# Graph message passing on one core: a tile of each pair made from columns on chip, joins in batches of twelve

## The reference

```python
msg_in = concatenate([nodes[row], nodes[col], edge_features], axis=-1)
messages = relu(msg_in @ mW1 + mb1) @ mW2 + mb2
aggregated = segment_sum(messages, col, num_segments=12500)
upd_in = concatenate([nodes, aggregated], axis=-1)
out = layernorm(nodes + relu(upd_in @ uW1 + ub1) @ uW2 + ub2)
```

## Time and profile before

| | us |
|---|---|
| median of 3 executions (2004.75 to 2006.22) | 2005.02 |
| the profiled execution | 2009.95 |
| its span, first to last instruction | 2008.1 |

### The profile page before, as it was taken

The page is one execution under the profiler, slowest core; times in us unless marked ns, Lnnn a source line. Parts: engine busy times, 40 slices in busy tenths (PEclk is TensorE's granted clock), DMA queues, the critical chain, the costliest instruction groups (busy, mean ns, idle before and its releaser), DMA issues.

```text
span 2008.1 us, 34318 instructions
## 1 busy us (share of the span) xinstructions
PE 1444.5 (72%) x8744; PEld 1325.3 (66%) x8744; DVE 1113.1 (55%) x4860; ACT 902.5 (45%) x6697; POOL 1479.6 (74%) x1576
## 2 busy tenths in 40 slices
PE   6866586777777666777667677768678767767778
PEld 6865575776667665667667666757667666666666
DVE  5545555555555555555555555555555555555553
ACT  3234453554454453454444444444444444444543
POOL 5677777777777777777777777777777777777773
PEclk9877777777777777877787778677776878787876
DMA  9554444444444444444344444445444444444441
GB/s 246 147 130 103 114 121 110 109 122 116 102 122 119 101 121 115 104 122 120 99 122 121 99 121 120 102 118 121 100 120 120 100 120 121 105 116 120 106 108 32
DMA packets 102730, 232.68 MB, mean 116 GB/s; under 512 B 47018, under 2 KB 63223, under 8 KB 89917
## 3 DMA queue, kind: packets, MB, share of 16 engines
q1 hardware_dynamic: 42532, 124.03, 24.4%
q0 software_dynamic: 49952, 100.83, 20.8%
q10 hardware_dynamic: 10046, 5.59, 1.2%
HBM read 220.66 MB, written 9.60 MB: 115 GB/s over the span
## 4 chain that ended last, share of the span: by engine, by line
POOL 73%; issue 24%; DMA 1%; PE 1%; POOLq 0%; ACT 0%; DVE 0%; DVEq 0%
POOL gath L798 71%; POOL hid L782 1%; DMA hid<-in_x_dram,idx_all 1%; POOL raw_x L782 1%; PE ps_sum L934 0%; DMA gath<-table_src,idx_all 0%; PE ps_pre L981 0%; PE ps_pre L987 0%; PE ps_pre L986 0%; PE ps_pre L997 0%; PE ps_pre L996 0%; POOLq L126 0%; DVE hid L1304 0%; PE ps_node L987 0%; PE ps_node L986 0%
## 5 line engine op out<-in xcount | busy, mean ns | idle before, releaser
L798 POOL DMA_INDIRECT gath<-table_src,idx_all x1513 | 1431.1, 946 | 461.4 <-issue 461.4
L914 PE MATMUL ps_pre<-rhs,lhs 128*128 128x128 f32 x3226 | 605.3, 365 | 531.7 <-DVE lhs L1275 529.0
L914 PEld LDWEIGHTS ps_pre<-rhs,lhs 128*128 128x128 f32 x3226 | 568.4, 273 | 549.3 <-DVE lhs L1275 546.3
L1304 DVE TENSOR_TENSOR hid<-ps_pre,gath 128x1024 f32<-128x1024 f32 x202 | 246.8, 1222 | 719.4 <-DMA gath<-table_src,idx_all 692.5
L520 ACT COPY col_x<-xz 64x1 f32 x5960 | 571.9, 189 | 3.3 <-issue 1.8
L934 PE MATMUL ps_sum<-onehot,hid 128*128 128x96 f32 x3322 | 482.1, 307 | 5.0 <-ACT hid L1105 3.4
L934 PEld LDWEIGHTS ps_sum<-onehot,hid 128*128 128x128 f32 x3322 | 462.5, 222 | 25.3 <-issue 19.5
L1105 ACT ACTIVATE hid<-hid 128x1024 f32<-128x1024 f32 x202 | 212.5, 1052 | 347.4 <-DVE hid L1304 347.2
L543 DVE TENSOR_TENSOR col_x<-xz 64x2 int32 x3366 | 264.2, 148 | 101.2 <-issue 98.5
L1275 DVE TENSOR_SCALAR_CACHE_REDUCE lhs<-lhs,place 96x1024 f32<-96x1024 int32 x208 | 262.5, 1262 | 14.6 <-DMA lhs<-in_dst_dram 14.6
L1067 ACT COPY rhs<-ps_sum 96x128 f32<-96x128 f32 x208 | 53.7, 259 | 354.0 <-DVE xz L1333 353.3
(11 more groups left out here) (136 smaller groups left out, 679.9 us busy)
## 6 DMA issues: line engine op xcount, KB each, us to landing
lhs<-in_dst_dram SPq DMA_DIRECT2D x99, 768.0 KB
lhs<-in_edgeT_dram SPq DMA_DIRECT2D x98, 256.0 KB
gath<-table_src,idx_all POOLq DMA_INDIRECT x1513
table_src<-gath SPq DMA_DIRECT2D x12, 512.0 KB, 8.0
xwin<-in_xT_dram SPq DMA_DIRECT2D x208, 24.0 KB
lhs<-in_dst_dram SPq DMA_DIRECT2D x10, 384.0 KB, 4.6
out_dram<-late_b ACTq DMA_DIRECT2D x48, 64.0 KB, 2.1
xz<-in_xT_dram ACTq DMA_DIRECT2D x4, 512.0 KB, 11.0
```

Source lines behind the costliest of these rows:

```text
L798: pool.indirect_dma_start(gath[0:m, k, j * H:(j + 1) * H], None, table_src, src_by_tile(p, j, m)).then_inc(gathered[k], 16)
L914: mm = nc.tensor.matmul(to[0:m, j * H:(j + 1) * H], lhs[:, k, j * P:j * P + m], rhs[:, k, :], start=True, stop=not by_cols)
L1304: nc.vector.tensor_tensor(hid[:, k, at], ps_pre[k % 2][:, at], gath[:, k, at], ALU.add).then_inc(hsum_made, 1)
```

## The change

Three things change together.

- From pair 11 on every pair has its last tile by columns (`COL_EVERY` 1), and of pairs 16, 20, ..., 204 tile 6 too (`TWO_FROM`, `TWO_EVERY`), in a buffer `col_y` of its own. The columns of tile 6 are put together over the four steps before: in each 8 by ScalarE and 24 by VectorE. Of tile 7 ScalarE now copies 56 and VectorE joins 72.
- VectorE's addition covers only the gathered tiles. ScalarE applies relu to the others straight from PSUM, and TensorE waits for that (`cols_relued`) before it writes that PSUM buffer again. The zeros are no longer needed.
- VectorE's joins come in batches of 12, each with a load of 24 registers: one after the addition, one after onehot, one after the comparison, and the one for tile 6 after the sums.

The column table gets a third plane. POOL's waits between the first six pairs' gathers are left out.

```diff
-COL_EVERY = 2
+COL_EVERY = 1
 COL_TILE = PT - 1
-COL_ACT = 60
-COL_LOADS = (12, 16, 12, 12, 8)
-COL_DVE = 32
+COL_ACT = 56
+COL_LOADS = (12, 16, 12, 8, 8)
+COL_JOINS = (24, 24, 24)
...
+TWO_FROM = 16
+TWO_EVERY = 4
+TWO_TILE = PT - 2
+TWO_STEPS = 4
+TWO_ACT = 8
+TWO_DVE = 24
+TWO_DVE_FROM = TWO_STEPS * TWO_ACT
...
+        col_f = sb("col_f", [P, 3 * TAB])
+        col_tab = sb("col_tab", [P, 3, P], I32)
         col_x = sb("col_x", [D, SLOTS, P])
+        col_y = sb("col_y", [D, 2, P])
...
+        def has_two(p):
+            return TWO_FROM <= p < LAST_PAIR and (p - TWO_FROM) % TWO_EVERY == 0
+        def two_ahead(p):
+            for part in range(TWO_STEPS):
+                if has_two(p + 1 + TWO_STEPS - part):
+                    return p + 1 + TWO_STEPS - part, part
+            return None
...
-            return rows_of(p) if is_last(p) else PT - has_cols(p)
+            return rows_of(p) if is_last(p) else PT - has_cols(p) - has_two(p)
+        def has_psum_rows(p):
+            return has_cols(p) and not is_last(p)
...
+        def load_two_regs(eng, p, start, count):
+            regs = [eng.alloc_register(f"col{next(col_regs)}") for n in range(count)]
+            eng.load(regs, col_tab[p // 2:p // 2 + 1, 2, start:start + count])
+            return regs
...
             pool.wait_ge(idx_first_in, 16)
             for r in range(RAW):
-                if r > 0:
-                    pool.wait_ge(raw_got[r - 1], 16 * PT)
                 for j in range(PT):
                     pool.indirect_dma_start(raw(r, j), None, x, src_by_tile(r, j, P)).then_inc(raw_got[r], 16)
...
                 pe.wait_ge(hsum_made, p - 1)
+                if has_psum_rows(p - 2):
+                    pe.wait_ge(cols_relued, col_batches(p - 2))
                 for j, m in tiles_of(p):
                     by_cols = has_cols(p) and (j == col_tile(p) or j == TILES and is_last(p))
+                    if has_two(p) and j == TWO_TILE:
+                        mm = nc.tensor.matmul(to[0:m, j * H:(j + 1) * H], lhs[:, k, j * P:j * P + m], rhs[:, k, :], start=True, stop=False)
+                        pe.wait_ge(two_act, TWO_STEPS * twos(p))
+                        pe.wait_ge(two_dve, TWO_STEPS * twos(p))
+                        mm = nc.tensor.matmul(to[0:m, j * H:(j + 1) * H], col_y[:, twos(p) % 2, 0:m], w_src[0:D, :], start=False, stop=True)
+                        continue
                     mm = nc.tensor.matmul(to[0:m, j * H:(j + 1) * H], lhs[:, k, j * P:j * P + m], rhs[:, k, :], start=True,
                                           stop=not by_cols)
                     if by_cols:
                         if j == col_tile(p):
                             pe.wait_ge(cols_act, col_batches(p) + is_last(p))
-                            pe.wait_ge(cols_dve, 2 * col_batches(p))
+                            pe.wait_ge(cols_dve, col_batches(p))
...
-                    pe.wait_ge(cols_listed, 2)
-                    for half in range(2):
+                    pe.wait_ge(cols_listed, 4)
+                    for half in range(3):
                         ins = nc.tensor.transpose(ps_node[0:TAB, half * P:(half + 1) * P], col_f[:, half * TAB:(half + 1) * TAB], ident[:, :])
...
             def relu(p, it, k):
                 act.wait_ge(hsum_made, p + 1)
-                h = hid[:, k, 0:rows_of(p) * H]
+                if has_psum_rows(p):
+                    at = slice(gathers_of(p) * H, PW)
+                    nc.scalar.activation(hid[:, k, at], ps_pre[k % 2][:, at], ACT.Relu).then_inc(cols_relued, 1)
+                h = hid[:, k, 0:gathers_of(p) * H]
                 nc.scalar.activation(h, h, ACT.Relu).then_inc(hid_made, 1)
...
                     held = act_regs.pop() + load_regs(act, p + 2, COL_LOADS[0], COL_LOADS[1])
-                    copy_batch(act, nc.scalar.copy, to, 0, held)
+                    copy_batch(act, nc.scalar.copy, col_x[:, to, :], 0, held)
                 window_at(it, k)
                 if has_cols(p + 2):
                     for count in COL_LOADS[2:]:
-                        done = copy_batch(act, nc.scalar.copy, to, start, load_regs(act, p + 2, start, count))
+                        done = copy_batch(act, nc.scalar.copy, col_x[:, to, :], start, load_regs(act, p + 2, start, count))
                         start += count
                     done.then_inc(cols_act, 1)
+                if two_ahead(p):
+                    q, part = two_ahead(p)
+                    held = load_two_regs(act, q, part * TWO_ACT, TWO_ACT)
+                    copy_batch(act, nc.scalar.copy, col_y[:, twos(q) % 2, :], part * TWO_ACT, held).then_inc(two_act, 1)
                 if p + 2 >= COL_FROM and has_cols(p + 3):
                     first_regs(p + 3)
...
                 dve.wait_ge(gathered[k], got(p))
-                if first_cols(p):
-                    dve.wait_ge(gath_zero, zeroed_before(p))
                 if is_last(p):
                     dve.wait_ge(last_made, len(LAST_TILES))
-                at = slice(0, rows_of(p) * H)
+                at = slice(0, gathers_of(p) * H)
                 nc.vector.tensor_tensor(hid[:, k, at], ps_pre[k % 2][:, at], gath[:, k, at], ALU.add).then_inc(hsum_made, 1)
-                if first_cols(p + SLOTS):
-                    dve.wait_ge(hsum_made, p + 1)
-                    nc.vector.memset(gath[:, k, COL_TILE * H:PW], 0.0).then_inc(gath_zero, 1)
...
+            def join_part(p, i):
+                if has_cols(p + 2):
+                    if i == 0:
+                        wait_cols(dve, p + 2)
+                    start = DVE_FROM + sum(COL_JOINS[:i])
+                    done = join_batch(col_x[:, (p + 2) % SLOTS, :], start, load_regs(dve, p + 2, start, COL_JOINS[i]))
+                    if i == len(COL_JOINS) - 1:
+                        done.then_inc(cols_dve, 1)
             def step(it, k):
                 if isinstance(it, int) and (it, k) == (1, 0):
                     relative(1)
+                p = it * SLOTS + k
                 before = pair(it, k, 1)
                 if before and not is_raw(before[0]):
                     add_gathered(*before)
+                join_part(p, 0)
                 if not (isinstance(it, int) and pair(it, k)[0] < 2):
                     onehots(*pair(it, k))
-                p = it * SLOTS + k
                 if p % SLOTS == SLOTS - 1:
                     load_starts(p - SLOTS + 1)
                 at = place_sums(p - 3) if p >= 3 else None
...
-                if has_cols(p + 1):
-                    to, start = (k + 1) % SLOTS, DVE_FROM + COL_DVE
-                    done = join_batch(col_x[:, to, :], start, load_regs(dve, p + 1, start, P - start))
-                    done.then_inc(cols_dve, 1)
-                if has_cols(p + 2):
-                    wait_cols(dve, p + 2)
+                join_part(p, 1)
                 after_this = pair(it, k, -1)
                 if after_this and after_this[0] >= 2:
                     turned(*after_this)
+                join_part(p, 2)
                 if pair(it, k, 3):
                     add_sums(*pair(it, k, 3), at)
-                if has_cols(p + 2):
-                    to = (k + 2) % SLOTS
-                    held = load_regs(dve, p + 2, DVE_FROM, COL_DVE)
-                    join_batch(col_x[:, to, :], DVE_FROM, held).then_inc(cols_dve, 1)
+                if two_ahead(p):
+                    q, part = two_ahead(p)
+                    start = TWO_DVE_FROM + part * TWO_DVE
+                    join_batch(col_y[:, twos(q) % 2, :], start, load_two_regs(dve, q, start, TWO_DVE)).then_inc(two_dve, 1)
```

More of the change, by code:

```diff
@@ L279, in gnn_kernel @@
         rings_made = sem("rings_made")
[L280 removed]
+        cols_relued = sem("cols_relued")
+        two_act = sem("two_act")
+        two_dve = sem("two_dve")
         gathered = [sem(f"gathered{i}") for i in range(SLOTS)]
@@ L457, in col_tile, with twos @@
             return LAST_ROWS if is_last(p) else COL_TILE
+        def has_two(p):
+            return TWO_FROM <= p < LAST_PAIR and (p - TWO_FROM) % TWO_EVERY == 0
+        def twos(p):
+            return sum(has_two(q) for q in range(p + 1))
+        def two_ahead(p):
[3 more added lines that the diff above has]
+            return None
         def gathers_of(p):
-            return rows_of(p) if is_last(p) else PT - has_cols(p)
+            return rows_of(p) if is_last(p) else PT - has_cols(p) - has_two(p)
+        def has_psum_rows(p):
+            return has_cols(p) and not is_last(p)
         def got(p):
@@ L471, in col_batches @@
             return sum(has_cols(q) for q in range(COL_FROM, p + 1))
-        def col_before(p):
-            return next((q for q in range(p - SLOTS, COL_FROM - 1, -SLOTS) if has_cols(q)), None)
-        def first_cols(p):
-            return has_cols(p) and col_before(p) is None
-        def zeroed_before(p):
-            return sum(first_cols(q) for q in range(p + 1))
         def two_of(p):
@@ L511, in column, with copy_batch @@
```

(14 more changed lines are left out.)

16 lines of the change are left out of this document (7 added, 9 removed).

## The result

The changed kernel takes 2027.26 us (median of nine runs, 2015.02 to 2032.15), the kernel before beside it 2006.22: the ratio is 1.0099, with a 95% interval of 1.0077 to 1.0121. It is 1% slower. The forecast was 1987 us and faster; the time lies within its range, on the side of the first rival. The profiled execution took 2026.47 us, its span is 2024.6.

A forecast was written before the change was run, and what follows sets the result against it. GpSimd's gathers were taken to bound the kernel at 9.38 us a pair, then VectorE's queue at 9.37; an earlier start and shorter end gave 18 us off the median of 2005.02, so 1987 us, range 1935 to 2045.

The forecast's parts named there:

- the first rival: VectorE's and ScalarE's register loads collide: one VectorE load of four 0.22 us longer, step 9.59, 2029 us; 22 in 100.
- The bound moves from GpSimd to VectorE's queue: From pair 11 on: the step goes from a POOL of 9.38 us to a VectorE queue of 9.37.
- POOL's floor of 8.44 us a step: GpSimd's gathers after the change: 6.75 a steady pair at 1.2505 us each, 0.94 us below before.
- The datapath at 7.5 us a step: VectorE's joins and other operations sum to 7.5 us a pair, without the queue's loads and issue.
- the shared port's rival: GpSimd shut out during VectorE's joins: 11.9 us a step, over 2470 us; 1 in 100.
- The queue's sum, 9.37: VectorE's queue a pair: loads 6.52, issue 2.24, and smaller terms for arithmetic, holes, window starts and node stage.
- Its note that each load lies behind a large operation: VectorE: each load follows a large operation and 12 joins, about 1.75 us of datapath work, hiding most of it.
- four loads of 24: 4 x 1.63 = 6.52: VectorE's queue: four 24-register loads a pair at 1.63 us each, bounds 1.5 and 1.85.
- The start: Up to pair 11: addition for pair 6 stays at 102.79, then 34.3 us to pair 11's at 137.1, not 151.5.
- The 0.60 for faster: Whole kernel: chance 0.60 that the change measures faster, against 0.10 the same and 0.30 slower.

The follow-up runs named there:

- the runs with 4 and 32 registers: Changed kernel with each VectorE batch load cut from 24 registers to 4, serving all 12 joins: 1802 us; or lengthened to 32, 8 of them unused: 2423 us.
- the layout in one half: Changed kernel with the seventh tile's table rows placed so VectorE and ScalarE nearly always load from the same half of the partitions: 1992.9 us, ratio to before 0.9926.
- half of the fourth batches: Changed kernel with TWO_EVERY 8, not 4, and table rows in the same half of the partitions: 1830.95 us, ratio to before 0.9125.
- opposite halves: Changed kernel with ScalarE's column-place loads all from partitions 0 to 63 and VectorE's from 64 to 95, so wrong columns are joined: 2001.7 us.
- the order that crowds them: Changed kernel with the three batches of a step side by side, no longer between VectorE's large operations: 2237 us.

## Why the prediction was wrong

- **The bound moves from GpSimd to VectorE's queue: right.** Shown by the runs with 4 and 32 registers. POOL's floor of 8.44 us a step is what the run with 4 registers reaches (8.39, with the lead at the start).
- **The datapath at 7.5 us a step, and the shared port's rival at 1 in 100: right.** VectorE is busy for 1568.7 us (near 1560 was forecast), ScalarE for 1559.2 (1580). Idle of "issue" ahead of joins is 348 us (350). TensorE's busy time rose by 197 us, not by 97, but it has 4% of the chain.
- **The queue's sum, 9.37: right as far as it went.** With nearly all loads of the short kind (the layout in one half) the segment takes 1809.8 us, where the prediction has 1813.5. Its terms are right together; of the single ones only the loads were measured. Its note that each load lies behind a large operation was the condition for that, worth 210 us.
- **The step that failed: "four loads of 24: 4 x 1.63 = 6.52".** It gave every load one duration. The mean was 1.690, 6.76 a step, because 189 of the 783 loads followed one from the other side of partition 64 and took 1.850 us, the others 1.639. The term was 0.24 us too small; the step came out 0.17 too long, the other terms together being some 0.07 too large. 0.17 us is nothing beside 9.4, but the forecast stood 0.09 us a step from its own sign, as its first rival says, and 0.17 us is paid 194 times: 32.9 of the 34.6 us. The layout in one half, which takes 162 of the long loads away, shortens the same stretch by 36.5 us (1846.3 to 1809.8).
- **The rival that came true in size was wrong in mechanism.** "Loads collide", one load in four by 0.22 us, 2029 us: the time came out so, and the share too (24%). That it came so near is luck: ScalarE has no part in it. The 20 long loads behind the earlier trace rows were put down to meetings with ScalarE. Sorted in time order, each of the 20 stands right behind VectorE's load of window starts. The 569 ns of a window-starts load among the 344 in the earlier trace rows was the same mark, read as scatter. Had the rule been read there, the change's new row table, p // 2 beside p % 105, would have shown how often the sides differ, and the load would have been 1.69 us from the start.
- **The start: right to 1.4 us,** though the addition for pair 6 did not stay at 102.79 but came at 105.59; the steps up to pair 11 were shorter instead (pair 7 follows after 3.77 us, where it was 9.88). The terms that it names for these steps add up to 34.1 us, not 34.3. **The 0.60 for faster** rested on a step known to about 0.1 us when a load had two durations 0.21 apart in the rows.
- **Open:** why executions of the changed kernel spread over 17 us, where those of the kernel before spread over 4.

## What to carry to other kernels

When a change moves work from a busy engine to one with idle time, cost the receiver's queue, not its busy time: register loads and issue stand in no busy column, and here they made a step of 9.5 us whose datapath needs 7.6 (1470.4 us of VectorE's busy time in 194 steps). When two engines come out within a few per cent, the sign is decided by the small scatter in the dearest repeated row: sort its long cases by what stands *before* them on the same queue, before blaming a neighbour. And take less of a change that overshoots: with the rows in one half, half of the fourth batches gave 9% where all of them gave under 1%.

## What was not expected of the hardware

- A register load on VectorE takes 0.21 us longer when that engine's load before it read from the other side of partition 64: 1.850 against 1.639 us for 24 registers, 0.570 against 0.350 for 4, 2.359 against 2.147 for 32. The surcharge is nearly the same for each length. ScalarE's loads have one of 0.17 to 0.18 us (0.976 against 0.798 for 12). Rows up to partition 104 were read.
- Loads of ScalarE at the same time did not matter: with opposite halves 558 of VectorE's loads beside one from the other half kept their 1.64 us.
- No load of VectorE began with more than 10 instructions (once 11) issued ahead of it and not yet started, in the order that crowds them (195 of 783 at exactly 10) and with 4 registers (440 at 10, ten at 11). A batch of 12 behind the large operations then held the next load back by about 1.4 us, an estimate from the step shown (its joins' issue some 0.5 us behind 1204.45, the load at 1206.4).
